# Eight cores, attention and a gated FFN: score products in pairs, and the start of the kernel reordered

## The reference

```
xn   = layernorm(x)                               # over the 1024 features, eps 1e-5
lat  = xn @ Wc_down                               # 1024 -> 512
q    = lat @ Wq_up                                # 512 -> 16 heads x 64
k, v = split(lat @ Wkv_up)                        # one head of 64, shared by all 16
s    = softmax(causal(q k^T / 8)) v @ Wc_proj     # 16 heads, 8192 positions
g    = silu(down(silu(gate(xn)) * up(xn)))        # hidden 3072, int weights / 127
out  = x + s * g
```

## Time and profile before

| | us |
|---|---|
| time, median of 3 runs | 1543.37 |
| lowest and highest run | 1540.68, 1683.09 |
| the profiled execution's own time | 1539.72 |
| its span on the slowest core (core 7) | 1538.2 |
| spans of the eight cores | 1525.6 to 1538.2 |
| TensorE (PE) busy | 1416.0 (92%) |
| ScalarE (ACT) busy | 1197.9 (78%) |
| VectorE (DVE) busy | 634.7 (41%) |
| GpSimd (POOL) busy | 340.1 (22%) |

### The profile page before, as it was taken

The page is one execution under the profiler, slowest core; times in us unless marked ns, Lnnn a source line. Parts: engine busy times, 40 slices in busy tenths (PEclk is TensorE's granted clock), DMA queues, the critical chain, the costliest instruction groups (busy, mean ns, idle before and its releaser), DMA issues.

```text
span 1538.2 us, 44936 instructions; the slowest of 8 cores (1525.6 to 1538.2 us)
## 1 busy us (share of the span) xinstructions
PE 1416.0 (92%) x18064; PEld 791.6 (51%) x18064; DVE 634.7 (41%) x1165; ACT 1197.9 (78%) x1254; POOL 340.1 (22%) x480
## 2 busy tenths in 40 slices
PE   2787999889899999999999999999999999999995
PEld 2554555555555554555555455555555555544442
DVE  4586666673636244251332333312233222134323
ACT  3555878778798989989999899899999999941110
POOL 3553433322121312142121100102130000111003
PEclk9898999989999999999999999999999999999998
DMA  9731423445454727366031122133132222345434
GB/s 237 147 112 56 105 79 95 105 112 117 119 117 117 160 65 189 106 132 159 33 114 63 50 70 71 38 116 111 50 118 70 70 64 83 112 145 195 156 121 157
DMA packets 67386, 166.78 MB, mean 108 GB/s; under 512 B 8048, under 2 KB 17520, under 8 KB 67184
## 3 DMA queue, kind: packets, MB, share of 16 engines
q1 hardware_dynamic: 54576, 132.31, 27.6%
q0 software_dynamic: 12608, 31.59, 11.4%
HBM read 152.47 MB, written 34.60 MB: 122 GB/s over the span
## 4 chain that ended last, share of the span: by engine, by line
PE 78%; issue 5%; DVE 5%; ACT 4%; DMA 4%; POOL 2%; SPq 0%; DVEq 0%; POOLq 0%; ACTq 0%
PE ps L226 77%; ACT p_sb L940 3%; DMA xt<-xb 3%; PE ps L237 2%; DMA wgu_sb<-wgub 1%; DVE bnd L566 1%; DVE g_sb L703 0%; DMA wdr<-wdb 0%; POOL acc_sb L859 0%; DVE h_sb L718 0%; DVE acc_sb L767 0%; DVE xn L409 0%; ACT xn L405 0%; POOL p_sb L947 0%; SPq L250 0%
## 5 line engine op out<-in xcount | busy, mean ns | idle before, releaser
L940 ACT ACTIVATE p_sb<-ps,nbias 128x1024 bf16<-128x1024 f32 x1024 | 1059.0, 1123 | 100.5 <-PE ps L226 83.4
L226 PE MATMUL ps<-vaug,p_sb 128*128 128x65 bf16 x8192 | 383.9, 194 | 21.5 <-DVE y_sb L990 14.2
L226 PEld LDWEIGHTS ps<-vaug,p_sb 128*128 128x128 bf16 x8192 | 306.5, 97 | 179.1 <-issue 147.6
L226 PE MATMUL ps<-own_f,wgu_sb 128*128 128x512 bf16 x1536 | 383.4, 382 | 10.7 <-DVE g_sb L703 3.4
L226 PE MATMUL ps<-qT,kT 64*128 64x256 bf16 (+1 forms) x4352 | 367.6, 271 | 14.4 <-DVE xnT L469 4.8
L226 PEld LDWEIGHTS ps<-qT,kT 64*128 64x128 bf16 x4352 | 150.6, 94 | 234.7 <-issue 204.1
L947 POOL TENSOR_TENSOR p_sb<-p_sb,mask_sb 128x512 bf16<-128x512 bf16 x64 | 74.2, 1160 | 622.0 <-ACT p_sb L940 621.9
L226 PEld LDWEIGHTS ps<-own_f,wgu_sb 128*128 128x128 bf16 x1536 | 131.2, 98 | 136.8 <-issue 24.2
L226 PE MATMUL ps<-wdr,h_sb 128*128 128x512 bf16 x768 | 192.8, 381 | 9.2 <-DMA wdr<-wdb 2.5
L703 DVE COPY g_sb<-ps 128x512 f32<-128x512 f32 x72 | 49.7, 691 | 173.5 <-PE ps L226 173.3
L226 PEld LDWEIGHTS ps<-wdr,h_sb 128*128 128x128 bf16 x768 | 64.6, 98 | 70.9 <-issue 17.5
(11 more groups left out here) (97 smaller groups left out, 1046.8 us busy)
## 6 DMA issues: line engine op xcount, KB each, us to landing
wgu_sb<-wgub SPq DMA_DIRECT2D x72, 512.0 KB, 3.3
xt<-xb SPq DMA_DIRECT2D x57, 512.0 KB, 5.4
wdr<-wdb SPq DMA_DIRECT2D x72, 256.0 KB, 5.3
wgu_sb<-wgu POOLq DMA_DIRECT2D x24, 512.0 KB, 6.9
wgub<-wgu_sb SPq DMA_DIRECT2D x24, 512.0 KB, 6.7
xo_t<-xo SPq DMA_DIRECT2D x32, 256.0 KB, 3.9
out<-acc_sb POOLq DMA_DIRECT2D x32, 256.0 KB, 4.4
wdr<-wd POOLq DMA_DIRECT2D x24, 256.0 KB, 7.7
```

The lines of the kernel that those rows point to most:

```text
L226: return p.op("tensor", lambda e: e.matmul(out, lhsT, rhs, start=start, stop=stop, skip_group_check=shared), waits, "pe" if tok else None, ...
L940: ex = A(cost, lambda en, dst=dst, src=src, bias=bias: en.activation(dst, src, AF.Exp, bias=bias, scale=0.125), [mm, p_prior(u)[1], bias_t ...
```

## The change

Six things are changed together.

- **Score batches.** A batch of one unit is offered only when it is the last unit of its slot (or of all). With two buffers the planner waits until both are free. A third unit is still added when its buffer is free at once.
- **Loads.** Wq is loaded as two halves with a semaphore each; x tiles 4 to 10 wait on the SP queue for the first half. The planner reckons 170 instead of 250 bytes/ns for SP's loads in the first 45 us.
- **LayerNorm of the first four groups.** Statistics and 1/sqrt go in twos in all four groups; the small operations go to VectorE if it is expected to be done first, else to GpSimd; the normalisation goes to ScalarE or VectorE, whichever is expected first. In all groups a normalisation is offered only when its 1/sqrt is expected to be ready.
- **Evictions of the first four groups and slots**, and of `gen_teff`, go to ScalarE or VectorE, whichever is expected first (`either`, `evict`). Masks of the first four slots go to VectorE if it is expected free ahead of GpSimd.
- **Order.** The last value products of a pass wait for the epilogue of the same half of the slot before; an epilogue waits for the projection two slots before; `down_end` looks again for a buffer for the spilled attention output in both of its forms.
- **Lead.** VectorE may be planned 2000 instead of 3000 ns ahead of TensorE during the first 16 tiles.

The diff, cut to its core:

```diff
+    FIRST = {"sync": 170.0, "gpsimd": 170.0}
...
+        def either(ca, emit_a, cv, emit_v, waits=()):
+
+            w = ready(*[t for t in waits if t is not None])
+            ta = max(p.T["scalar"], w) + ca + p.LAT["scalar"]
+            tv = max(p.T["vector"], w) + cv + p.LAT["vector"]
+            return A(ca, emit_a, waits) if ta < tv else V(cv, emit_v, waits)
...
-            x_tok[j] = DMA(x_tile(j), xb_d[j * 128:(j + 1) * 128, :], f"x{q}", 512, [x_free.get(q)])
+            x_tok[j] = DMA(x_tile(j), xb_d[j * 128:(j + 1) * 128, :], f"x{q}", 512, [x_free.get(q), after])
...
-        t_wq = DMA(wq_sb[:, :, :], wq_d.ap().rearrange("(k p) m -> p k m", p=128), "w_q", 2048, engine="gpsimd")
+        wq_v = wq_d.ap().rearrange("(k p) m -> p k m", p=128)
+        t_wqs = [DMA(wq_sb[:, 2 * i:2 * i + 2, :], wq_v[:, 2 * i:2 * i + 2, :], f"w_q{i}", 1024, engine="gpsimd")
+                 for i in range(2)]
+
         for j in range(4, 11):
-            load_x(j)
+            load_x(j, t_wqs[0])
...
+            S, c = P, 230
+            if shared and p.T["vector"] + 10 * 270.0 < max(p.T["gpsimd"], agg.t) + 12 * 380.0:
+                S, c = V, 160
...
-                yield lambda j=j: 0.0 if j < 4 or j - 4 in tp_done else INF
+                yield lambda j=j, a=a: ready(a) if j < 4 or j - 4 in tp_done else INF
...
-            yield from ln_tiles(0, 2)
-            yield from ln_tiles(2, 2)
-            for g in range(1, NG):
+            for j in range(0, 4 * PRO, 2):
+                yield from ln_tiles(j, 2)
+            for g in range(PRO, NG):
                 yield from ln_tiles(4 * g, 4)
...
-                    ex = P(1350, lambda en, mk=mk: en.tensor_tensor(
+                    on_v = e < PRO and p.T["vector"] < p.T["gpsimd"]
+                    ex = (V if on_v else P)(500 if on_v else 1150, lambda en, mk=mk: en.tensor_tensor(
...
+            if last and e > 0 and (e - 1, hg // 2) not in epi_done:
+                return INF
...
-            yield lambda: max(ready(yt), bank_t())
+            yield lambda: max(ready(yt), bank_t(), 0.0 if e < 2 or e - 2 in proj_done else INF)
...
-                    elif p.T["vector"] <= now() + (400.0 if len(xn_tok) >= 4 * PRO else 3000.0) and w.at() <= now() + 400.0:
+                    elif p.T["vector"] <= now() + (400.0 if len(xn_tok) >= 4 * PRO else 2000.0) and w.at() <= now() + 400.0:
...
-                    if n >= (2 if nbuf == 3 else 1) and tn > t0:
+                    if n >= 2 and tn > t0:
                         break
                     at = max(at, tn)
                     n += 1
-                if n:
+                if n >= 2 or n and (nu + n == NU or units[nu + n][0] > units[nu][0]):
                     offer(at, ("s", n))
```

More of the change, by code:

```diff
@@ L247, in P, with evict @@
             return p.op("gpsimd", emit, waits, "g", cost)
+        def either(ca, emit_a, cv, emit_v, waits=()):
[3 more added lines that the diff above has]
+            return A(ca, emit_a, waits) if ta < tv else V(cv, emit_v, waits)
+        def evict(g, dst, src, waits, ca=600, cv=690):
+            on_v = lambda e: e.tensor_copy(dst, src)
+            if g >= PRO:
+                return V(cv, on_v, waits)
+            return either(ca, lambda e: e.activation(dst, src, AF.Copy), cv, on_v, waits)
         def DMA(dst, src, sem, kb, waits=(), engine="sync"):
@@ L351, in gen_teff @@
                 ms = slice(4 * hf, 4 * hf + 4)
+                evs = []
+                on_a = p.T["scalar"] < p.T["vector"]
                 for out, col in ((teffk[:, ms, 0:64], 0), (teffk[:, ms, 64:128], 0), (teffv[:, ms, :], 64)):
                     src = tf_v[:, :, col:col + 64]
[L354 to L359, removed]
+                    evs.append(A(350, lambda e, out=out, src=src: e.activation(out, src, AF.Copy), [mm]) if on_a else
+                               V(350, lambda e, out=out, src=src: e.tensor_copy(out, src), [mm]))
+                give(b, evs)
+                teff_tok.extend(evs)
             h_free.append(mm)
@@ L397, in ln_tiles @@
-            shared = j0 < 4 * PRO
+                a = S(c, lambda e: e.tensor_tensor(t, y, y, ALU.mult), [a])
+                a = S(c, lambda e: e.tensor_tensor(t, t, v, ALU.mult), [a])
+                a = S(c, lambda e: e.tensor_scalar(t, t, -0.5, 1.5, ALU.mult, ALU.add), [a])
+                a = S(c, lambda e, dst=dst: e.tensor_tensor(dst, t, y, ALU.mult), [a])
             if shared:
-                a = P(230, lambda e: e.tensor_tensor(t, mv[:, js, 0], rstd[:, js], ALU.mult), [a])
-                a = P(230, lambda e: e.tensor_scalar(nmr[:, js], t, -1.0, None, ALU.mult), [a])
+                a = S(c, lambda e: e.tensor_tensor(t, mv[:, js, 0], rstd[:, js], ALU.mult), [a])
@@ L545, in gen_q @@
                                 latT[:, k, :], k == 0, k == LK - 1,
-                                [lev, t_wq] + fr if m4 == 0 and k == 0 else [],
+                                [lev] + t_wqs + fr if m4 == 0 and k == 0 else [],
                                 tok=(m4 == 3 and k == LK - 1))
@@ L839, in down_end @@
                 fetch(e, nh)
-                if (e, nh) not in fetched and (e, nh) in s_spill:
-                    yield lambda: INF if held[r] else 0.0
-                    fetch(e, nh)
+            yield lambda: 0.0
+            if (e, nh) not in fetched and (e, nh) in s_spill:
+                yield lambda: INF if held[r] else 0.0
+                fetch(e, nh)
             direct = (e, nh) in fetched
-            yield lambda: 0.0
             sm = av if bd is None else bank(bd)
@@ L924, in emit_scores @@
                                 qT[r0:r0 + 64, par, 2 * hg:2 * hg + 2, lo:128], True, True,
-                                fr + [k_tok[t // 4], q_tok[e]] if tt == 0 and o == 0 else [],
+                                fr + [k_tok[t // 4]] + q_tok[e] if tt == 0 and o == 0 else [],
                                 tok=(tt == 1 and o == 1), cost=w / 1.2 if o else 2.0)
@@ L1014, in build_program @@
         s_free = [None, None]
+        proj_done = set()
+        epi_done = set()
         def gen_proj(e):
@@ L1046, in gen_proj @@
             yT_free[par] = mm
+            proj_done.add(e)
         class Work:
```

65 lines of the change are left out of this document (31 added, 34 removed).

## The result

The changed kernel is faster, but by much less than forecast: ratio 0.988 to the kernel before (95% interval 0.9855 to 0.9912), about 1524 us in undisturbed executions (1523.2 and 1523.4) against 1542. The forecast was 1496 us (range 1476 to 1532): the direction and the range held, the size did not, 18 us gained where 47 were promised.

What follows compares the result with a forecast made beforehand. Behind the start, TensorE's needed time plus 66 us of idle pieces was taken as the bound. Terms -38.6 + 0 + 5 - 6 - 7 = -46.6 took the profiled 1539.7 to 1493; the median lies 3.7 higher: 1496 us, range 1476 to 1532.

Steps and rivals of the forecast that it cites:

- Part 1: Score products, 60 to 1360 us: 193 fewer runs at 0.20 us of TensorE each, -38.6 us (ends 0 and -42).
- Part 2: Attention: 0.85 us idle ScalarE per two-buffer pair, 119 us for 140 pairs; TensorE price 0, covered by the FFN.
- Rival C: ScalarE becomes the bound, the two-buffer state spreads and attention outlasts the FFN: 1598 us, slower; chance 0.07.
- Part 3: TensorE's waits for the second exponential under its fixed order: +5 us, ends 0 and +31.
- Rival B: Saved switches come back as waits, +31 us at the upper end: 1536, about 1525 taken; chance 0.20.
- Part 4: Loads at the start: x tiles 4 to 10 held, weights land earlier; -6 us up to 100 us, ends +10 and -14.
- Part 5: First groups: short work goes where expected first, no normalisation ahead of its square root; -7 us, ends +8 and -14.
- the loss to contention: Masks on VectorE stop GpSimd through a shared SBUF port: up to 19 us of GpSimd, a third reaching TensorE.
- The row taken as agreement: GpSimd's square of q took 2.34 us against 1.92 mean beside four VectorE normalisations; read as agreeing with the shared-port rule.
- The y_sb wait near 140 us: TensorE's 6.33 us wait at 139.82 for a late y_sb, forecast to be gone in the changed profile.
- likeliest case: Rival A, the forecast itself: TensorE-bound, removed runs pay in full, 1496 us; chance 0.68.
- each cover: FFN work that fills TensorE while ScalarE is slower: about 157 us thick before, about 120 with pairs.

Runs made afterwards that it cites:

- the hold alone: Kernel before with only x tiles 4 to 10 behind half of Wq, Wq in halves, slower reckoning of first loads: 1519 us, ratio 0.988.
- changed, unpaired: Changed kernel with the old rule for score batches, the other five parts kept: 1539 us, ratio 0.997.
- VectorE's copies: Changed kernel without VectorE's copy of the gate product to SBUF while two score buffers are in use in slots 0 to 7: 1523 us, ratio 0.990.

## Why the prediction was wrong, by its own steps

**Part 1, scores in pairs (-38.6).** The mechanism is right: 206 runs fewer where 193 were forecast. The price was too high: 0.165 to 0.17 us by TensorE's busy time, 0.18 by the device time, not 0.20. The score matmuls' own busy time fell from 367.6 to 334.1 us, -33.5 or 0.16 a run. TensorE's whole busy time agrees on the two profiled cores: -33.0 and +4.4 for the clock make the -28.6. The price had been read from medians of chosen neighbours; doubling the count of runs was the measurement that a few rows could not replace.

**Part 2, what pairs cost ScalarE (0).** Right in its unit price: in a two-buffer stretch of the changed kernel ScalarE stands 0.86 and 0.77 us before a pair, 0.85 forecast,

```profile
240.85 2.12 ACT L961 ACTIVATE p_sb<-ps,nbias 128x1024 bf16<-128x1024 f32 x2 [0.86 <-PE ps L228]
...
243.74 2.12 ACT L961 ACTIVATE p_sb<-ps,nbias 128x1024 bf16<-128x1024 f32 x2 [0.77 <-PE ps L228]
```

and attention ended near 1465 us. The 119 us for all pairs were too many: ScalarE's idle time in 60 to 1360 us grew by 79. Rival C, attention outliving the FFN, did not come about. But "covered by the FFN, price 0" is the step that failed in kind. The FFN did fill TensorE; it did not fill it for nothing. It came forward into 160 to 600 us, and where pairs stand on the hold alone TensorE's waits there grew for about ten producers. The FFN was also cut into more pieces: with pairs in the changed kernel its matmuls stand in 578 runs in place of 432 and are busy 597 us in place of 574 (means over the cores), of which the clock is at most 3.

**Part 3, waits (+5, ends 0 and +31).** This is the term that was mis-sized. It priced one producer, the second exponential (8.7 to 22.0 us, +13.3), and forgot that a different order moves every other wait too. Measured over all producers, this is what pairs change, in us, as means over the eight cores of the profiled executions (idle up to TensorE's last matmul, busy without the clock's share, all rounded):

| pairs added to | runs | busy | clock | idle | behind the last matmul | span |
|---|---|---|---|---|---|---|
| changed, unpaired | -204 | -31 | +3 | +17 | -5 | -16 |
| before | -198 | -25 | +11 | +21 | -4 | +3 |
| before, hold | -204 | -27 | +9 | +38 | -4 | +15 |

The score matmuls alone give back 33 to 34 us in each row; the other products take some of it again, the FFN's 23 to 30 us more, the rest 17 to 18 less. So +20 to +47 of idle time and clock stand where the forecast had +5. Rival B, the saved switches coming back as waits, had been given 0.20 and a price of up to 31; for pairs by themselves it is what happened, in two of three settings completely. That the whole change still landed within the stated range is owed to the hold, which brought more than its share.

**Part 4, the loads (-6).** Wc came at 19.9 us (18.5 forecast, 22.8 before) and the first scores at 47.2 (52 forecast). Its worth was mis-sized the other way: -20 us alone (1519 against 1539), 16 in the changed kernel, beyond the end of -14. None of it is seen at the start: idle time and clock up to 160 us sum to 61.5 us before and 61.3 with the hold alone (means of the cores). It comes later: idle time from 160 to 600 us goes down from 29 to 19 us and the clock's share there from 5 to 2, and behind 600 us another 4 us of idle time go. The forecast had reasoned from the start alone. Why the order behind the start has fewer waits is not shown by any run here.

**Part 5, engines and lead (-7).** With fixed engines the changed kernel is at 0.992, with the small operations on GpSimd at 0.994: 0 to -9, so the -7 is neither confirmed nor refuted. Only 12 of the 32 masks went to VectorE, and the loss to contention that was to take this part to -1 is not seen: with all masks on GpSimd the kernel is not faster. The row taken as agreement, four normalisations beside one square, has operations with one tensor input and is a weak instance of that rule. The y_sb wait near 140 us is gone, as forecast, and another of 5.9 us stands at 62.22. The parts do not add: without pairs, all that the change has beside the hold (twos, engines, evictions, order, lead) takes the ratio from 0.988 to 0.997, 15 us slower; with pairs it takes it from 0.997 to 0.988, 14 us faster. The forecast's sum assumed that they add.

So on the new start -31 of busy time, +15 for what comes back and for the end, -4 for the other five parts: -20, where 18 were measured and single executions scatter by a few us. The prediction took its likeliest case at full gain because each cover was thick enough on average; here, under a fixed order, a cover thick enough on average did not keep TensorE from waiting.

**What stays open.** Which of the many small delays comes first when the FFN is drawn forward; the one candidate tried, VectorE's copies, is out. Why the hold lowers waits behind 160 us, and why the other parts lose time without pairs and gain it with them, is open too.

## What to carry to other kernels

Price a repeated overhead by changing its count in an otherwise equal kernel; rows read next to chosen neighbours gave a fifth too much. Where one program fixes the order on every engine, a change that shifts the balance between two streams of work changes all waits: give it a term for the whole idle time, of the size of the gain, and shift an estimate slightly to see how much of a small difference is the plan. Test the parts of a bundle apart: here one wait on a queue was worth as much as the whole bundle, and the part with the best arithmetic was worth nothing on its own.

## What the runs showed of the hardware that was not expected

A small operation of VectorE stretches under a mask multiply on GpSimd. Timeline of the changed kernel near 57 us: a tensor_scalar on 128 x 2 takes 0.93 us while GpSimd multiplies 128 x 512, and 0.17 us alone at 60.45.

```profile
57.51 1.18 POOL L969 TENSOR_TENSOR p_sb<-p_sb,mask_sb 128x512 bf16<-128x512 bf16 x1 [2.11 <-ACT p_sb L961]
57.52 0.16 DVE L416 TENSOR_TENSOR nw<-nw 128x2 f32<-128x2 f32 x1
57.78 0.93 DVE L417 TENSOR_SCALAR nw<-nw 128x2 f32<-128x2 f32 x1
...
60.45 0.17 DVE L417 TENSOR_SCALAR nw<-nw 128x2 f32<-128x2 f32 x1
```

That is an operation with one tensor input; the one just before it, with two, took 0.16 us although it began with the mask multiply. The case of the rule that the prediction weighed (the Trainium skill, "SBUF — State Buffer", section "Who interferes with whom"), two inputs in SBUF, is a mask on VectorE: 0.89 us beside a mask multiply on GpSimd, 0.42 us alone.

```profile
51.89 0.42 DVE L969 TENSOR_TENSOR p_sb<-p_sb,mask_sb 128x512 bf16<-128x512 bf16 x1 [0.44 <-ACT p_sb L961]
...
54.25 1.15 POOL L969 TENSOR_TENSOR p_sb<-p_sb,mask_sb 128x512 bf16<-128x512 bf16 x1 [0.59 <-ACT p_sb L961]
...
54.79 0.89 DVE L969 TENSOR_TENSOR p_dg<-p_dg,mask_sb 128x512 bf16<-128x512 bf16 x1 [0.36 <-ACT p_dg L961]
```

All eight masks of this kind that VectorE ran beside one on GpSimd took 0.88 to 0.90 us, the four without one 0.42 to 0.43. So the trace agrees with the rule, and here VectorE is the one that stands. It is no large cost: taking these operations off VectorE made the kernel no faster.
